# Attention scores of two heads issued side by side, with a ring of four for the split probabilities

## The chip, the cores and the metric

The kernel runs on one core of a Trainium2 chip. The metric is the time of one execution in microseconds. The engines that matter here are TensorE (PE in the profile; PEld is its weight load), VectorE (DVE), ScalarE (ACT), GpSimd (POOL) and the DMA queue that SyncE (SP) feeds. Each engine takes its instructions in the order in which they are written; semaphores tie the engines together.

## What is computed

One layer of a vision transformer over 32 images of 256x256 (the rows are the tokens), with a class token in front, so that 257 tokens of width 256 stand for an image:

- tokens: a three-level Haar transform, gates from dot products with all coefficients, and the inverse transform;
- attention with 16 heads of width 64: `qkv = layernorm(x) @ w_qkv`, rotary embedding on q and k, `scores = q @ k^T / sqrt(192)` plus a slope per head times the distance and a causal mask, softmax, `softmax @ v`, output projection, residual;
- a feed-forward part of width 1024 whose activations and weights are rounded to integers: `silu(gate) * up`, then `down`, residual.

```
scores = jnp.einsum('bhqd,bhkd->bhqk', q, k) / jnp.sqrt(jnp.float32(f))
...
out = bitlinear(silu(bitlinear(x, w_gate)) * bitlinear(x, w_up), w_down)
```

## The kernel before, in words

The first transposes XT start 147 us into the span; from there the program is a pipeline over images. A step works on four images at once: stage A makes the tokens of image s+1 (synthesis, layer norm, transposes XT), stage B the q, k and v of image s, stage C the attention of image s-1, stage E the output projection and the feed-forward part of image s-1. A step has 16 slots, k = 0 to 15, and each engine runs the same slots with its own share of each. Steps 4 to 29 are a hardware loop of 13 passes with two steps each; the others are written out.

The order is written by hand, by tables of slots: QK_SLOT = 1, 2, 3, 4, 5, 7, 8, 9 (one group of two head pairs of q or k each), V_SLOT = 10 to 13, SYN_SLOT = 6 (the synthesis of stage A, L774), OP_PARTS = slots 2 and 3 (output projection), H2_SLOT = 4 and XQ_SLOT = 5 (residual, layer norm and token scale on DVE), GU_SLOT = 7, 8, 10, 12 (gate and up), Q2T_SLOT = 11, 14, DOWN_SLOT = 14, 15.

One head of the attention takes this way, with k its slot:

- PE, slot k-2: `scores` (L706 to L714), two f32 matmuls of 64 rows each, 129 columns (the first 128 queries) and 257 columns (the other 128), into the bank `s_bank[h % 2]`. Even heads have their q and k on partitions 0 to 63, odd heads on 64 to 127. It waits (`t_done`) until DVE has evicted the two heads before.
- DVE, slot k-2: `ttr` (L1043), two instructions at L1055 that add the bias, write to `tp[:, h % 4]` and leave the maximum in `nm`. It waits for `s_ready`.
- ACT, slot k-2: `exps` (L501 on), two exponentials (L509) in place.
- PE, slot k: `transposes` (L720), three f32 transposes (L726) into one of the two banks `pt_bank`. ACT, slot k: `pt_hi` copies them to f16 (`ptr_h`, L514); DVE, slot k: `pt_lo` writes the f16 remainder (`ptr_l`, L1060). `ptr_h` and `ptr_l` have two buffers, `h % 2`.
- PE, slot k+1: `values` (L740), nine f16 matmuls of 64 columns (L624) into `o_bank`. It waits for `pt_free`, which `pt_lo` raises, and for the first head of a group of four for `ao_ready`.
- DVE, slots 4, 8, 12 and 0: `normalise` (L1070), the reciprocal (L1073) and the multiplication of four heads (L1079) out of `o_bank`. PE, slots 6, 10, 14 and 2: `out_transposes` (L731), four transposes of them (L735) through `pt_bank`.

The QK and V matmuls all use one bank, `b_bank`: the next group waits (`rq_ready`, `vl_done`) until ACT (L501, rows `rq`) or ACT and DVE (L560, L1169) have evicted the last. `output`, `quantise_tokens` (L1093 to L1104) and `norm_stats` (L1082) are further DVE work in the slots named. In a slot PE's order is: XT or synthesis, scores, QK or V, transposes of xq, transposes of the head, output projection, values, gate and up, `out_transposes`, down, transposes of q2.

Of the kernel before, what the change touches and what calls it, by code (L numbers as in the profile page):

```python
# [27 lines left out]
F16 = mybir.dt.float16  # L28
# [25 lines left out]
AHEAD = 2  # L54
BANDS, OPS, TERMS, BLOCK = 10, 4, 3, 8
# [52 lines left out]
def vit_layer(nc, x, cls_tok, Wa, ba, Wd1, bd1, Wd2, bd2, Wd3, bd3, w_qkv, b_qkv, w_out, b_out,  # L108
              w_gate, w_up, w_down, c_cos, c_sin, c_rel, c_mask, c_row, c_avg, c_eye, out):
    with ExitStack() as ctx:  # L110
# [69 lines left out]
        ptr_h = sb("ptr_h", [P, 2, 3, P], F16)  # L180
        ptr_l = sb("ptr_l", [P, 2, 3, P], F16)
# [317 lines left out]
        def _(act):  # L499
# [16 lines left out]
            def pt_hi(c, h, start):  # L516
                if not start or h >= 2:
                    act.wait_ge(pv_done, 16 * c + h - 1)
                use = pt_use(h, start)
                hi_of(c, use, ptr_h[:, h % 2], pt_bank[use % 2][:, 0:3 * P].rearrange("p (b n) -> p b n", b=3))  # L520
# [99 lines left out]
        def _(pe):  # L620
# [86 lines left out]
            def scores(c, h, par, start):  # L707
                half = slice(64 * (h % 2), 64 * (h % 2) + 64)
                if not start or h >= 2:
                    pe.wait_ge(t_done, 32 * c + 2 * h - 2)  # L710
                j = h // 2
                bank = s_bank[h % 2]
                pe.matmul(bank[:, 0:W0], qt[par][half, j, 0:P], kt[par][half, j, 0:W0], start=True, stop=True)  # L713
                pe.matmul(bank[:, W0:SCOLS], qt[par][half, j, P:SIDE], kt[par][half, j, :], start=True, stop=True).then_inc(s_ready, 1)  # L714
# [23 lines left out]
            def values(c, h, par, start):  # L738
# [6 lines left out]
                for t in range(T):  # L745
                    dst = o_bank[:, t * SIDE + (h % 4) * DH:t * SIDE + (h % 4 + 1) * DH]
                    blocks = [(0, 0)] if t == 0 else [(1, 0), (2, 1)]
                    for n, (pb, kb) in enumerate(blocks):
                        ins = split3(dst, (ptr_h[:, h % 2, pb, :], ptr_l[:, h % 2, pb, :]),
# [3 lines left out]
            def step(s, par):  # L753
# [3 lines left out]
                for k in range(SLOTS):  # L757
# [19 lines left out]
                    if ahead:  # L777
                        if ahead[1] == 0:
                            pe.wait_ge(qk_done, 8 * s + 8)
                        scores(ahead[0], ahead[1], par if ahead[1] < AHEAD else cp, ahead[2])  # L780

# [49 lines left out]
                    if has_c and k >= 1:  # L831
                        values(c, k - 1, cp, start)
                    if has_e and not start and k == 0:
                        values(c - 1, HEADS - 1, par, False)
# [37 lines left out]
        def _(dve):  # L872
# [189 lines left out]
            def pt_lo(c, h, start):  # L1062
                use = pt_use(h, start)
                lo_of(c, use, ptr_l[:, h % 2], pt_bank[use % 2][:, 0:3 * P].rearrange("p (b n) -> p b n", b=3), ptr_h[:, h % 2])
# [55 lines left out]
            def step(s, par):  # L1120
# [5 lines left out]
                for k in range(SLOTS):  # L1126
                    ahead = head_ahead(s, k)
                    if ahead:
                        ttr(*ahead)
                    if k == 0 and has_e and not start:  # L1130
# [47 lines left out]
                    if has_c and k >= 4 and k % 4 == 0:  # L1178
# [91 lines left out]
```

## Time and profile before

| | |
|---|---|
| median of 3 runs | 2515.66 us (2510.66 to 2520.93) |
| the profiled execution | 2511.47 us, of which span 2509.7 us |
| busy, share of the span | PE 84%, PEld 59%, DVE 70%, ACT 54%, POOL 41% |
| mean granted TensorE clock | 0.926 |

A step takes about 69 us, and 75 us where the loop turns back in it. A line of groups gives the line of the kernel, the engine, the operation, what it writes and reads, the count, the busy time, the mean of one in ns, and the idle time before it with what ended it. A matmul of f32 data shows as two records, and its end is modelled, so starts are the better measure of PE.

### The profile page before, as it was taken

To read this page: it belongs to the slowest core of one execution; us is meant where nothing else is said; L and a number is where in the kernel's file an instruction comes from. 1 tells how busy PE (TensorE), PEld (TensorE's weight loads), DVE (VectorE), ACT (ScalarE), POOL (GpSimd) and SP (SyncE) were. 2 spreads that over 40 slices of the span, in tenths; PEclk is the share of its full clock that TensorE was granted. 3 is DMA by queue.
4 is the path that set the end of the run, shared out by engine and by line. 5 is a ranking of instruction groups with operands and counts; after the bars stand their busy time and mean duration, and the time that the engine had idled before them with its cause. 6 is when DMAs were issued, how large, how long until landed. Compare 5 with 4: busy or idle time off the path is not lost.

```text
span 2509.7 us, 55124 instructions
## 1 busy us (share of the span) xinstructions
PE 2097.1 (84%) x16742; PEld 1478.4 (59%) x16742; DVE 1747.1 (70%) x5024; ACT 1366.7 (54%) x3841; POOL 1019.9 (41%) x1098
## 2 busy tenths in 40 slices
PE   3658889888888898888888888889888888888885
PEld 2535666666566665655656666656666655566653
DVE  2537777767777676768767676777767677777764
ACT  0125665556555555656656565655655565556653
POOL 0155543434455444434554353455534344554400
PEclk7789999999899999989999999899989999999976
DMA  7311111111111111111111111111111111111100
GB/s 174 122 47 39 44 48 43 39 39 44 36 39 47 49 46 38 41 36 37 43 48 48 38 45 36 39 38 45 47 43 40 38 43 39 39 47 43 43 9 9
DMA packets 98172, 114.84 MB, mean 46 GB/s; under 512 B 22721, under 2 KB 60066, under 8 KB 97570
## 3 DMA queue, kind: packets, MB, share of 16 engines
q1 hardware_dynamic: 97826, 110.61, 17.1%
q8 instruction: 170, 2.79, 0.5%
q14 instruction: 176, 1.44, 0.2%
HBM read 26.62 MB, written 8.42 MB: 14 GB/s over the span
## 4 chain that ended last, share of the span: by engine, by line
PE 38%; issue 23%; DVE 20%; ACT 9%; POOL 6%; SPq 2%; DVEq 1%; ACTq 0%; DMA 0%; POOLq 0%
PE bank L624 17%; PE bank L714 4%; PE bank L774 4%; PE bank L713 3%; PE bank L726 3%; DVE th L1202 2%; PE bank L858 2%; DVE arena L1206 2%; DVE es L1209 2%; ACT arena L509 2%; DVE ptr_l L1060 2%; DVE arena L1055 2%; POOL arena L484 2%; POOL rot L480 2%; PE bank L735 1%
## 5 line engine op out<-in xcount | busy, mean ns | idle before, releaser
L480 POOL TENSOR_TENSOR rot<-rot,sin 128x512 f32<-128x512 f32 x256 | 328.7, 1284 | 1176.4 <-DMA rot<-rq 1176.1
L509 ACT ACTIVATE arena<-arena,nm 128x129 f32<-128x129 f32 (+1 forms) x1024 | 458.4, 455 | 193.2 <-DVE nm L1055 192.9
L1055 DVE CUSTOM_DVE_ANT_0 arena<-bank,bias 128x129 f32<-128x129 f32 (+1 forms) x1024 | 323.9, 354 | 206.4 <-PE bank L714 190.8
L624 PE MATMUL bank<-xt_h,weights 128*128 128x256 f16 x2048 | 404.7, 285 | 8.4 <-ACT rq L501 5.8
L501 ACT ACTIVATE rq<-bank,bqk 128x256 f32<-128x256 f32 x512 | 214.8, 471 | 343.2 <-PE bank L624 337.0
L514 ACT ACTIVATE ptr_h<-bank 128x384 f16<-128x384 f32 x512 | 250.0, 488 | 220.3 <-PE bank L726 220.0
L484 POOL TENSOR_TENSOR arena<-arena,rot 128x256 f32<-128x256 f32 (+1 forms) x384 | 346.9, 918 | 30.3 <-POOL rot L480 0.5
L624 PE MATMUL bank<-arena,ptr_h 128*128 128x64 f16 x3072 | 215.0, 198 | 162.2 <-DVE ptr_l L1060 155.4
L1060 DVE TENSOR_TENSOR ptr_l<-bank,ptr_h 128x384 f16<-128x384 f32 x512 | 281.1, 549 | 55.5 <-ACT ptr_h L514 54.9
L714 PE MATMUL bank<-arena 64*128 64x257 f32 x1024 | 319.2, 393 | 0.0
L624 PEld LDWEIGHTS bank<-arena,ptr_h 128*128 128x128 f16 x3072 | 189.4, 101 | 195.2 <-DVE ptr_l L1060 181.6
L624 PE MATMUL bank<-xt_l,weights 128*128 128x256 f16 x1024 | 291.0, 284 | 0.0
L713 PE MATMUL bank<-arena 64*128 64x129 f32 x1024 | 258.3, 334 | 38.4 <-issue 36.4
L624 PEld LDWEIGHTS bank<-xt_h,weights 128*128 128x128 f16 x2048 | 207.3, 101 | 127.8 <-issue 85.9
L726 PE MATMUL bank<-eye,arena 128*128 128x128 f32 x1536 | 271.1, 287 | 0.0
L1174 DVE TENSOR_TENSOR arena<-rq,cos 128x256 f32<-128x256 f32 (+1 forms) x192 | 134.6, 727 | 173.2 <-ACT rq L501 173.2
L713 PEld LDWEIGHTS bank<-arena 64*128 64x128 f32 x1024 | 157.2, 192 | 148.3 <-issue 130.5
L726 PEld LDWEIGHTS bank<-eye,arena 128*128 128x128 f32 x1536 | 188.0, 146 | 77.4 <-issue 40.7
L624 PE MATMUL bank<-weights,xt_h 128*128 128x512 f16 x512 | 156.3, 387 | 58.1 <-DVE arena L1169 56.4
L509 ACT ACTIVATION_READ_ACCUMULATOR arena<-arena,nm 128x1 f32 x1024 | 202.2, 197 | 0.0
L624 PE MATMUL bank<-arena,ptr_l 128*128 128x64 f16 x1536 | 198.3, 198 | 0.0
L624 PE MATMUL bank<-weights,arena 128*128 128x256 f16 x1536 | 178.3, 273 | 1.9 <-DVE arena L1060 1.5
(187 smaller groups left out, 3766.2 us busy)
## 6 DMA issues: line engine op xcount, KB each, us to landing
rot<-rq SPq DMA_DIRECT2D x1024, 64.0 KB, 2.0
arena<-in_x SPq DMA_DIRECT2D x4, 2048.0 KB, 18.2
xin<-in_x SPq DMA_DIRECT2D x32, 256.0 KB, 2.7
hr<-hr SPq DMA_DIRECT2D x32, 256.0 KB, 2.4
out<-h SPq DMA_DIRECT2D x64, 128.0 KB, 1.7
arena<-in_L_attn_w_qkv SPq DMA_DIRECT2D x2, 1536.0 KB, 6.4
arena<-in_L_attn_w_out SPq DMA_DIRECT2D x1, 1024.0 KB, 10.1
arena<-in_L_ffn_w_gate SPq DMA_DIRECT2D x1, 1024.0 KB, 6.5
```

The source lines that it names most:

```text
L480: pool.tensor_tensor(r, r, sin[:, :].unsqueeze(1).broadcast_to([P, 2, SIDE]), ALU.mult).then_inc(t2_ready, 1)
L484: ins = pool.tensor_tensor(dst, dst, rot[:, g % 2, :, cols], ALU.add)
L501: return act.activation(dst, src, ACT.Identity, **kw)
L509: act.activation(cols, cols, ACT.Exp, bias=nm[:, t, h:h + 1], scale=-1.0, accum_out=rs[:, t, h:h + 1]).then_inc(e_done, 1)
L514: act.activation(dst, src, ACT.Copy).then_inc(hi_done, 1)
L624: ins = pe.matmul(dst, lhs[l], rhs[r], start=start and n == 0, stop=stop and n == len(parts) - 1)
L713: pe.matmul(bank[:, 0:W0], qt[par][half, j, 0:P], kt[par][half, j, 0:W0], start=True, stop=True)
L714: pe.matmul(bank[:, W0:SCOLS], qt[par][half, j, P:SIDE], kt[par][half, j, :], start=True, stop=True).then_inc(s_ready, 1)
L726: ins = pe.transpose(pt_bank[use % 2][:, n * P:(n + 1) * P], r[:, col:col + P], eye[:, :])
L1055: dve.tensor_tensor_reduce(r[:, cols], bank[:, cols], b, -1.0, 3.0e38, ALU.add, ALU.min, nm[:, t, h:h + 1]).then_inc(t_done, 1)
L1060: tt(dst, src, hi, ALU.subtract).then_inc(pt_free, 1)
L1174: ins = tt(dst, rq[:, g % 2, :, r], cos[:, r].unsqueeze(1).broadcast_to([P, 2, r.stop - r.start]), ALU.mult)
```

## The change

It has two parts. (1) `scores` becomes `score_pair`: in even slots PE issues both heads of a pair, 129 columns of each half and then 257 columns of each half, after one wait; DVE's `ttr` for both stands in the even slot too. ACT's exponentials stay one head a slot. (2) `ptr_h` and `ptr_l` have four buffers instead of two, `values` of head h stands in slot h+2 instead of h+1, and `normalise` moves one slot later, to 5, 9, 13 and 1. `out_transposes` stay in slots 6, 10, 14 and 2.

```diff
@@ -52,6 +52,7 @@
 V_SLOT = [10, 11, 12, 13]
 BEFORE_SYN = sum(k < SYN_SLOT for k in QK_SLOT)
 AHEAD = 2
+RING, LAG = 4, 2
 BANDS, OPS, TERMS, BLOCK = 10, 4, 3, 8
 FACTORS = OPS * TERMS
 Z_COLS = 4
@@ -177,8 +178,8 @@
         nm = sb("nm", [P, T, HEADS])
         rs = sb("rs", [P, T, HEADS])
         rinv = sb("rinv", [P, T, 4])
-        ptr_h = sb("ptr_h", [P, 2, 3, P], F16)
-        ptr_l = sb("ptr_l", [P, 2, 3, P], F16)
+        ptr_h = sb("ptr_h", [P, RING, 3, P], F16)
+        ptr_l = sb("ptr_l", [P, RING, 3, P], F16)
         ao = sb("ao", [P, 2, T, 4 * DH])
 
         h2 = sb("h2", [P, 2, T, SIDE])
@@ -514,10 +515,10 @@
                 act.activation(dst, src, ACT.Copy).then_inc(hi_done, 1)
 
             def pt_hi(c, h, start):
-                if not start or h >= 2:
-                    act.wait_ge(pv_done, 16 * c + h - 1)
+                if not start or h >= RING:
+                    act.wait_ge(pv_done, 16 * c + h - RING + 1)
                 use = pt_use(h, start)
-                hi_of(c, use, ptr_h[:, h % 2], pt_bank[use % 2][:, 0:3 * P].rearrange("p (b n) -> p b n", b=3))
+                hi_of(c, use, ptr_h[:, h % RING], pt_bank[use % 2][:, 0:3 * P].rearrange("p (b n) -> p b n", b=3))
 
             def at_hi(c, g, last=False):
                 if not first(c):
@@ -704,14 +705,14 @@
             pe.wait_ge(prep_done, 1)
             pe.wait_ge(turned_copied, 6)
 
-            def scores(c, h, par, start):
-                half = slice(64 * (h % 2), 64 * (h % 2) + 64)
-                if not start or h >= 2:
-                    pe.wait_ge(t_done, 32 * c + 2 * h - 2)
-                j = h // 2
-                bank = s_bank[h % 2]
-                pe.matmul(bank[:, 0:W0], qt[par][half, j, 0:P], kt[par][half, j, 0:W0], start=True, stop=True)
-                pe.matmul(bank[:, W0:SCOLS], qt[par][half, j, P:SIDE], kt[par][half, j, :], start=True, stop=True).then_inc(s_ready, 1)
+            def score_pair(c, j, par, start):
+                halves = slice(0, 64), slice(64, 128)
+                if not start or j >= 1:
+                    pe.wait_ge(t_done, 32 * c + 4 * j)
+                for half, bank in zip(halves, s_bank):
+                    pe.matmul(bank[:, 0:W0], qt[par][half, j, 0:P], kt[par][half, j, 0:W0], start=True, stop=True)
+                for half, bank in zip(halves, s_bank):
+                    pe.matmul(bank[:, W0:SCOLS], qt[par][half, j, P:SIDE], kt[par][half, j, :], start=True, stop=True).then_inc(s_ready, 1)
 
             def wait_bank(c, use, start):
                 if not start or use >= 2:
@@ -746,7 +747,7 @@
                     dst = o_bank[:, t * SIDE + (h % 4) * DH:t * SIDE + (h % 4 + 1) * DH]
                     blocks = [(0, 0)] if t == 0 else [(1, 0), (2, 1)]
                     for n, (pb, kb) in enumerate(blocks):
-                        ins = split3(dst, (ptr_h[:, h % 2, pb, :], ptr_l[:, h % 2, pb, :]),
+                        ins = split3(dst, (ptr_h[:, h % RING, pb, :], ptr_l[:, h % RING, pb, :]),
                                      (vh[par][:, kb, feat], vl[par][:, kb, feat]), n == 0, n == len(blocks) - 1)
                 ins.then_inc(pv_done, 1)
 
@@ -774,10 +775,10 @@
                             ins = pe.matmul(b_bank[:, :], rowop[:, o, :], rhs, start=o == 0, stop=o == OPS - 1)
                         ins.then_inc(syn_ready, 1)
                     ahead = head_ahead(s, k)
-                    if ahead:
+                    if ahead and k % 2 == 0:
                         if ahead[1] == 0:
                             pe.wait_ge(qk_done, 8 * s + 8)
-                        scores(ahead[0], ahead[1], par if ahead[1] < AHEAD else cp, ahead[2])
+                        score_pair(ahead[0], ahead[1] // 2, par if ahead[1] < AHEAD else cp, ahead[2])
 
                     if has_b and k in QK_SLOT:
                         g = QK_SLOT.index(k)
@@ -828,10 +829,10 @@
                                              (wo_h[:, j, :], wo_l[:, j, :]), j == 0, j == PAIRS - 1)
                         if k == 3:
                             ins.then_inc(op_ready, 1)
-                    if has_c and k >= 1:
-                        values(c, k - 1, cp, start)
-                    if has_e and not start and k == 0:
-                        values(c - 1, HEADS - 1, par, False)
+                    if has_c and k >= LAG:
+                        values(c, k - LAG, cp, start)
+                    if has_e and not start and k < LAG:
+                        values(c - 1, HEADS - LAG + k, par, False)
                     if has_e and k in GU_SLOT:
                         n = GU_SLOT.index(k)
                         t, half = n // 2, n % 2
@@ -1061,7 +1062,7 @@
 
             def pt_lo(c, h, start):
                 use = pt_use(h, start)
-                lo_of(c, use, ptr_l[:, h % 2], pt_bank[use % 2][:, 0:3 * P].rearrange("p (b n) -> p b n", b=3), ptr_h[:, h % 2])
+                lo_of(c, use, ptr_l[:, h % RING], pt_bank[use % 2][:, 0:3 * P].rearrange("p (b n) -> p b n", b=3), ptr_h[:, h % RING])
 
             def at_lo(c, g, last=False):
                 feat = slice(2 * g, 2 * g + 2)
@@ -1125,8 +1126,9 @@
                 ce.begin(e)
                 for k in range(SLOTS):
                     ahead = head_ahead(s, k)
-                    if ahead:
+                    if ahead and k % 2 == 0:
                         ttr(*ahead)
+                        ttr(*head_ahead(s, k + 1))
                     if k == 0 and has_e and not start:
                         output(e - 1, 1 - ep, 1)
                     if has_e and k - 1 == DOWN_SLOT[0]:
@@ -1175,9 +1177,9 @@
                         ins.then_inc(t1_done, 1)
                     if has_c:
                         pt_lo(c, k, start)
-                    if has_c and k >= 4 and k % 4 == 0:
+                    if has_c and k >= 4 and k % 4 == LAG - 1:
                         normalise(c, k // 4 - 1)
-                    if has_e and not start and k == 0:
+                    if has_e and not start and k == LAG - 1:
                         normalise(c - 1, 3)
 
                     if has_a and k == SYN_SLOT:
```

The built program shows what this does on PE around slots 4 and 5 of a step (L713 and L714, now L713 and L715, are score matmuls; L726, now L727, transposes of a head; `bank<-arena,ptr_h` and `ptr_l` values; `xt_h` and `xt_l` the q and k projection; REGISTER_ALU rows prepare a wait). Before, from the transposes of slot 4 to the projection of slot 5:

```order
L726 MATMUL bank<-eye,arena 128x128 x3
L739 REGISTER_ALU
L624 MATMUL bank<-arena,ptr_h 128x64 x2
L624 MATMUL bank<-arena,ptr_l 128x64
L624 MATMUL bank<-arena,ptr_h 128x64 x2
L624 MATMUL bank<-arena,ptr_l 128x64
L624 MATMUL bank<-arena,ptr_h 128x64 x2
L624 MATMUL bank<-arena,ptr_l 128x64
L710 REGISTER_ALU
L713 MATMUL bank<-arena 128x129
L714 MATMUL bank<-arena 128x257
L789 REGISTER_ALU
```

Now, from the last values of slot 3 to the projection of slot 4, and then the boundary from slot 4 to slot 5:

```order
L625 MATMUL bank<-arena,ptr_l 128x64
L625 MATMUL bank<-arena,ptr_h 128x64 x2
L625 MATMUL bank<-arena,ptr_l 128x64
L711 REGISTER_ALU
L713 MATMUL bank<-arena 128x129 x2
L715 MATMUL bank<-arena 128x257 x2
L790 REGISTER_ALU
L625 MATMUL bank<-xt_h,weights 128x256
```

```order
L727 MATMUL bank<-eye,arena 128x128 x3
L625 MATMUL bank<-arena,ptr_h 128x64 x2
L625 MATMUL bank<-arena,ptr_l 128x64
L625 MATMUL bank<-arena,ptr_h 128x64 x2
L625 MATMUL bank<-arena,ptr_l 128x64
L625 MATMUL bank<-arena,ptr_h 128x64 x2
L625 MATMUL bank<-arena,ptr_l 128x64
L790 REGISTER_ALU
L625 MATMUL bank<-xt_h,weights 128x256
```

The scores of head 7 have left the boundary and stand with those of head 6 in front of the projection of slot 4, so that in slot 5 the projection follows the values directly.

On DVE, slots 4 and 5 (L1055, now L1056, is the eviction of scores; L1060, now L1061, `ptr_l`; L1096, now L1097, the start of the token scale). Before, from the normalisation's neighbour to the token scale:

```order
L1059 REGISTER_ALU
L1060 TENSOR_TENSOR ptr_l<-bank,ptr_h 128x384
L1072 ISA
L1073 RECIPROCAL rinv<-rs 128x8
L1078 REGISTER_ALU
L1079 TENSOR_TENSOR ao<-bank,rinv 128x512
L1046 REGISTER_ALU
L1055 ISA arena,nm<-bank,bias 128x129
L1055 ISA nm 128x1
L1055 ISA arena,nm<-bank,bias 128x257
L1055 ISA nm 128x1
L1096 TENSOR_SCALAR th<-h,mv,rstd 128x256 x2
```

Now the residual follows two evictions, and the token scale follows `ptr_l`:

```order
L1056 ISA arena,nm<-bank,bias 128x257
L1056 ISA nm 128x1
L1047 REGISTER_ALU
L1056 ISA arena,nm<-bank,bias 128x129
L1056 ISA nm 128x1
L1056 ISA arena,nm<-bank,bias 128x257
L1056 ISA nm 128x1
L1155 SCALAR_TENSOR_TENSOR h<-bank,hr 128x512
```

```order
L1060 REGISTER_ALU
L1061 TENSOR_TENSOR ptr_l<-bank,ptr_h 128x384
L1097 TENSOR_SCALAR th<-h,mv,rstd 128x256 x2
L85 REGISTER_ALU
L1099 TENSOR_REDUCE es<-th 128x2
```

The second eviction has moved ahead of the residual (L1153, now L1155), and the normalisation from in front of the token scale to behind it, beside the evictions of slot 6.

## Rows read from the trace of the kernel before

**Rows 1.** Page: busy time of the engines; the chain by engine.
```profile
PE 2097.1 (84%) x16742; PEld 1478.4 (59%) x16742; DVE 1747.1 (70%) x5024; ACT 1366.7 (54%) x3841; POOL 1019.9 (41%) x1098
...
PE 38%; issue 23%; DVE 20%; ACT 9%; POOL 6%; SPq 2%; DVEq 1%; ACTq 0%; DMA 0%; POOLq 0%
```

**Rows 2.** Stretches of one step: window, length, busy us of PE, PEld, DVE, ACT, POOL; clock, DMA.
```profile
1187.92:1203.79 15.87, 15.87 (x153) 13.25 (x153) 8.91 (x28) 8.44 (x29) 6.51 (x5) 1.00 0.29 79
1203.79:1210.14 6.35, 5.86 (x59) 4.63 (x57) 4.87 (x19) 3.05 (x10) 4.47 (x4) 1.00 0.20 46
1210.14:1216.51 6.37, 5.87 (x29) 2.95 (x29) 6.20 (x14) 2.43 (x10) 5.20 (x6) 1.00 0.38 93
...
1221.45:1253.41 31.96, 26.02 (x205) 17.31 (x205) 27.42 (x76) 20.69 (x57) 13.53 (x17) 0.95 0.11 25
...
1259.97:1266.80 6.83, 6.83 (x32) 4.69 (x33) 3.05 (x12) 1.36 (x5) 0.00 (x0) 0.50 0.18 62
```

**Rows 3.** PE in order of time: start, us, engine, line, operation, count.
```profile
1197.07 0.19 PE L624 MATMUL bank<-arena,ptr_l 128*128 128x64 f16 x1
1197.09 0.63 PE L735 MATMUL bank<-eye,ao 128*128 128x128 f32 x4
...
1203.67 0.19 PE L624 MATMUL bank<-arena,ptr_l 128*128 128x64 f16 x1
1203.79 0.49 PE L713 MATMUL bank<-arena 64*128 64x129 f32 x2
1204.12 0.60 PE L714 MATMUL bank<-arena 64*128 64x257 f32 x2
1204.64 0.28 PE L624 MATMUL bank<-xt_h,weights 128*128 128x256 f16 x1
...
1205.97 0.49 PE L726 MATMUL bank<-eye,arena 128*128 128x128 f32 x3
...
1210.14 1.12 PE L774 MATMUL bank<-xin,rowop 128*128 128x512 f32 x2 [0.49 <-ACT rq L501]
```

**Rows 4.** The chain of waits through the same step: start, us, what.
```profile
1210.14 3.69 PE bank L774 x8
...
1256.91 3.05 issue
1259.96 0.57 PE bank L713
```

**Rows 5.** ACT in order of time.
```profile
1206.17 0.84 ACT L501 ACTIVATE rq<-bank,bqk 128x256 f32<-128x256 f32 x2 [3.89 <-PE bank L624]
```

**Rows 6.** DVE in order of time.
```profile
1204.93 0.29 DVE L1055 CUSTOM_DVE_ANT_0 arena<-bank,bias 128x129 f32<-128x129 f32 x1 [1.93 <-PE bank L714]
...
1205.49 0.69 DVE L1153 SCALAR_TENSOR_TENSOR h<-bank,hr 128x512 f32<-128x512 f32 x1
...
1208.08 0.19 DVE L1073 RECIPROCAL rinv<-rs 128x8 f32<-128x8 f32 x1
...
1209.00 0.28 DVE L1055 CUSTOM_DVE_ANT_0 arena<-bank,bias 128x129 f32<-128x129 f32 x1
...
1209.55 0.73 DVE L1096 TENSOR_SCALAR th<-h,mv,rstd 128x256 f32<-128x256 f32 x2
...
1215.07 0.54 DVE L1060 TENSOR_TENSOR ptr_l<-bank,ptr_h 128x384 f16<-128x384 f32 x1
...
1242.89 0.69 DVE L1169 SCALAR_TENSOR_TENSOR arena<-bank,arena 128x512 f16<-128x512 f32 x1 [1.18 <-ACT arena L560]
```

**Rows 7.** PE at the step's end, in order of time.
```profile
1249.72 0.29 PE L624 MATMUL bank<-arena,ptr_h 128*128 128x64 f16 x2 [1.87 <-DVE ptr_l L1060]
...
1252.79 0.79 PE L865 MATMUL bank<-eye,q 128*128 128x128 f16 x8
...
1255.86 1.05 PE L858 MATMUL bank<-wdn,q2t 128*128 128x256 f16 x8 [0.26 <-ACT q2t L543]
```

**Rows 8.** Waits over the whole span: us in total, times, longest.
```profile
PE bank L624 <- DVE ptr_l L1060: 155.4, 88, 2.8
```

## The prediction, made before the changed kernel was run

> **What bounds the kernel now.** I read the page's busy shares and chain first. PE is busy 84% and DVE 70% of the span, and the chain that ended last is PE for 38%, DVE for 20% and "issue" for 23% [rows 1]: the two take turns. So I cut one step of the steady state into stretches [rows 2]. In slots 0 to 3 (1187.92 to 1203.79) PE is busy all of its 15.87 us while DVE works 8.91: a saved PE microsecond is a saved microsecond. In slots 4 and 5 PE still has 5.86 of 6.35. From the synthesis to slot 7 DVE works 6.20 of 6.37, beside 5.87 of PE. In slots 8 to 14 DVE works 27.42 of 31.96 and PE waits in pieces; there PE time is worth little, and what matters is what stands in DVE's queue ahead of what PE and ACT wait for. The step here is 69.0 us (slot 0 to slot 0, 1187.92 to 1256.92), then comes the loop's turn with 3.05 us in which nothing runs [rows 4].
>
> **What a score set costs.** The last value matmul in front of a set starts at 1203.67, at a pace of 0.03; the first projection behind it starts at 1204.64 [rows 3]. So a head costs PE 1204.64 - 1203.70 = 0.94 us. The pure streaming is less: the synthesis takes 3.69 us for 8 records of 512 columns [rows 4], 0.90 ns a column and record, and a head has 2 x (129 + 257) = 772 of them: 0.69 us. The other 0.25 is entering and leaving. What that is shows by its neighbour: four f32 transposes over all 128 rows follow the last value matmul after 0.02 us (1197.07 to 1197.09), the 64-row scores only after 0.12 (1203.67 to 1203.79), and behind them stands a gap of the same kind [rows 3]. The Trainium skill, "TensorEngine Tiling (Array Packing)", section Tiling Modes, says that a change of tiling mode drains the array and a change of tile does not; the trace agrees as far as the mode goes, and shows no change of tile alone.
>
> A pair costs 1.88 now. Bounds for it after the change:
> - At least the entering and leaving of one head goes: 0.25 saved. That is the end without any overlap of the two halves. Below it the trace gives nothing but the gap: if each of the three changes of half costs the 0.1 of that gap, nothing is saved.
> - At most the second head disappears behind the first: 0.94 saved.
> I take 0.55. Each matmul is two records on the same 64 rows, in the order A A B B (129 columns), A A B B (257): only where a record of one half follows one of the other can they overlap, which is 0.12 + 0.12 + 0.23 of the 0.69; weights have to be loaded between them too, so I take 0.3 of it, plus 0.25.
> The Trainium skill, "TensorE: Matmul & The Clock Gate", Part 3, says that matmuls in different row groups run together with starts about 4 ns apart. By that rule the pair would come near the 0.94 end, which is the third rival below; no row here shows two halves next to each other.
>
> **The sum for one step,** in the order of time, gains positive.
> - Slots 0 to 3: two pairs, 2 x 0.55 = **+1.1**. With all of it PE-bound, it arrives. The output projection waits for DVE's remainder of the last `out_transposes`, which keeps its distance.
> - Slot 5: new wait. The projection there needs ACT's eviction of the slot before, which starts 0.2 after the projection ends (1205.97 to 1206.17) and takes 0.84 [rows 3, 5]. Now only transposes and values (about 0.6) stand between, no scores: PE stops for 0.4. The third pair in slot 4 pays it (0.55), and the synthesis waits for its own eviction as now (0.49) [rows 3].
> - Slots 4 to 7, DVE: **-0.9**. The residual (1205.49) now stands behind a second eviction of 0.56 (1204.93 to 1205.49), whose scores also end later. In front of the token scale the normalisation (1208.08 to 1209.00, 0.92) and one eviction (0.55) are gone, but it needs POOL's root, so it starts at about the same distance, and it ends with the `ptr_l` of 1215.07 [rows 6]. Then the 0.92 of the normalisation stands in front of the evictions of slot 6, hence of ACT's exponentials and its rounding of the tokens behind them. PE's values and `out_transposes` in slot 6 wait for it too, about as long as PE now waits there for `ptr_l`.
> - Slots 8 to 13, DVE-bound: **-0.2**. The normalisation moves from slot 8, where ACT's exponentials and tanh hid it, into slot 9 and delays the first V remainder by 0.9. In slot 11 no eviction stands ahead of the second one any more, and the wait of 1.18 for the third [rows 6] shrinks to about half: 0.7 comes back.
> - Slots 14 and 15: **+0.5**. Values now wait for a `ptr_l` that is long done, so the stop of 1.87 at 1249.72 [rows 7] goes. In its place `out_transposes` wait for the normalisation, now in slot 13 and about 2 us after the inner scale, where this `ptr_l` is 1.7 after it; but DVE's evictions and `q2` go on meanwhile, and the transposes of q2 (1252.79) start about 0.5 earlier.
> - Slot 15 loses a whole score set on PE, and that is worth **0**: the down product behind it already waits 0.26 for ACT's copy of q2t [rows 7], and will wait 1.2.
> Sum: 1.1 - 0.9 - 0.2 + 0.5 = 0.5 us a step, 16 us over 32 steps. After the loop's turn PE's granted clock is 0.50, the 1.2 GHz level, for 6.83 us [rows 2], in which the first pair falls, so there it saves twice as much: 13 turns x 0.55 = 7 us. From the profiled execution's own 2511.5 us (span 2509.7 and 1.8 around it; the median of the runs, 2515.7, is 4 higher) that gives 2488; I say **2490 us**. With the pair at 0.25 the first term is 0.5 and the step -0.1; with 0.94 it is 1.9 and the step 1.3: 2511 to 2463 with little or nothing from the turns.
>
> **Rivals.**
> - *The halves take turns* (the pair saves 0.25 or nothing). For it: no row shows two matmuls of 64 rows overlapping, and f32 matmuls come as two dependent records. Against: nothing in the trace. Then the gain of slots 0 to 3 is eaten by slots 4 to 7: -0.1 a step, about 2512 us. No change.
> - *Evictions in pairs get in DVE's way* (slower). The place is DVE's queue in slots 4, 8, 10 and 12, where 0.56 of the next head's eviction, not needed before ACT's next slot, stands ahead of work that PE and ACT wait for, together with 0.92 of normalisation in slots 9 and 13. For it: 27.42 of 31.96 busy there. Against: total work on DVE is unchanged, and what is done early is not done later. If half of the four evictions (1.1) shows on top of my -0.2 and the end gives 0 instead of 0.5, the step is 1.1 lower than my sum: 1.1 - 0.9 - 1.3 = -1.1, and the pairs of the loop's turn give 7 back: about 2539 us at worst, 2530 as its middle. It decides as soon as these delays exceed 0.5 a step.
> - *Both parts give more.* The halves overlap nearly in full, 1.9 in slots 0 to 3 and slots 4 to 6 follow, and the waits of values for `ptr_l`, 155.4 us in 88 pieces [rows 8], leave the path in other places than slot 14 too. For it: values are what PE stops for most. Against: most of those pieces lie where DVE is the bound, and PE only stops for something else. At 2 us a step: 2445 us.
>
> **How the numbers follow.** Forecast 0.33, turns 0.23, slower 0.22, more 0.22. What this measurement can tell from no change is about 0.5%, 12.6 us: faster is below 2503, slower above 2528. Faster: 0.29 of the forecast, all of the third rival, 0.02 of the first: 0.53. Same: 0.04 + 0.18 + 0.02 of the slower one = 0.24. Slower: 0.23. The forecast's own range is 2463 to 2511. The range of 8 in 10 reaches down to the third rival and up to the middle of the slower one with a little more: 2432 to 2534.
>
> **What would show it.** The starts in slot 4: from the last value matmul to the first projection about 1.36 us for two heads (1.67 if they take turns, 1.0 if in full overlap). In slot 5 a stop of PE for ACT's `rq` of about 0.4. The row of values waiting for `ptr_l` falls from 155 us to near nothing, and rows of `out_transposes` or values waiting for `ao` grow. The evictions of slot 6 come about 1.5 after the token scale's end instead of at once. In slot 15 the down product waits about 1.2 for q2t. DVE's and ACT's busy times stay. I am wrong if slots 0 to 3 don't get shorter by about 1, or if slots 8 to 14, now 32 us, change by more than 1 in either direction; and if PE, with longer stops, is granted 1.2 GHz more often than the 0.95 of the last stretch [rows 2] shows now.

## The result, and the profile after

The changed kernel takes 2550.8 us (median of 4, 2550.3 to 2555.0) against 2518.3 us before (2510.7 to 2526.5): a ratio of 1.013, interval 1.010 to 1.017. It is slower, where 2490 us and faster was forecast, and 17 us above the range. Its two parts taken alone pull in opposite directions: the pairs alone give 2418 us, the lag alone (values two slots behind, normalisation one slot later) 2609 us. The two don't add up: -3.7% and +3.7% are no change, and +1.3% was measured.

The page, in the order of [rows 1]:

```profile
PE 1940.9 (76%) x16742; PEld 1399.2 (55%) x16742; DVE 1797.6 (71%) x5024; ACT 1373.3 (54%) x3841; POOL 1028.5 (40%) x1098
...
issue 49%; POOL 21%; DVE 15%; PE 9%; ACT 2%; SPq 2%; POOLq 1%; DMA 1%; DVEq 0%; ACTq 0%
```

PE does the same 16742 matmuls in 156 us less busy time, and the kernel is slower all the same. The chain reads quite differently from [rows 1] (PE 9%, "issue" 49%, POOL 21%). Half of it names no wait, so I do not use it as a guide. DVE does the same 5024 instructions in 50 us more, though its busy time was forecast to stay; more on this below. The stretches of one step are (slots 0 to 3, 4 and 5, synthesis to slot 8, slot 8 to XT):

```profile
1209.09:1223.06 13.97, 13.97 (x154) 12.23 (x153) 8.39 (x26) 8.43 (x29) 5.44 (x4) 1.00 0.30 80
1223.06:1228.97 5.91, 5.00 (x59) 4.17 (x57) 4.21 (x16) 3.05 (x10) 4.62 (x5) 1.00 0.18 42
1228.97:1242.14 13.17, 10.81 (x64) 6.39 (x64) 10.18 (x28) 7.00 (x20) 8.37 (x9) 0.87 0.20 51
1242.14:1276.73 34.59, 27.15 (x210) 17.95 (x209) 29.02 (x81) 20.97 (x57) 13.63 (x17) 0.81 0.10 23
```

Against [rows 2]: slots 0 to 3 went from 15.87 to 13.97 us, 1.9 less, and slots 4 and 5 from 6.35 to 5.91. Then the gain is given back, with interest: slot 8 to XT had 31.96 and has 34.59 now, 2.6 more, and its granted clock fell from 0.95 to 0.81. From synthesis to slot 8 it is 13.17 against 11.31 (1210.14 to 1221.45), 1.9 more, at 0.87.

Where it happens is plain on PE in slot 10 of a step. Before the change, with the V product of slot 11 at the end:

```profile
1232.75 0.23 PE L624 MATMUL bank<-arena,ptr_h 128*128 128x64 f16 x2 [2.00 <-DVE ptr_l L1060]
...
1233.02 1.03 PE L845 MATMUL bank<-wgu,xqt 128*128 128x512 f16 x4
...
1236.09 0.61 PE L624 MATMUL bank<-weights,xt_h 128*128 128x512 f16 x2 [0.76 <-DVE arena L1169]
...
1237.40 0.49 PE L726 MATMUL bank<-eye,arena 128*128 128x128 f32 x3
```

and after it:

```profile
1250.23 0.49 PE L727 MATMUL bank<-eye,arena 128*128 128x128 f32 x3
1254.19 0.27 PE L625 MATMUL bank<-arena,ptr_h 128*128 128x64 f16 x2 [3.47 <-DVE ao L1080]
...
1254.64 1.90 PE L846 MATMUL bank<-wgu,xqt 128*128 128x512 f16 x4
...
1258.21 1.04 PE L625 MATMUL bank<-weights,xt_h 128*128 128x512 f16 x2 [0.82 <-DVE arena L1171]
...
1260.74 0.85 PE L727 MATMUL bank<-eye,arena 128*128 128x128 f32 x3
```

The values of head 8 wait 3.47 us for `ao`, the normalisation of heads 4 to 7. After it PE works at half clock: the gate and up products take 1.90 instead of 1.03, the V product of slot 11 takes 2.53 (1258.21 to 1260.74) instead of 1.31 (1236.09 to 1237.40). The granted clock of the stretch is 0.50, the 1.2 GHz level:

```profile
1254.19:1260.74 6.55, 5.73 (x23) 2.75 (x24) 6.48 (x17) 2.16 (x6) 5.61 (x6) 0.50 0.00 0
```

The trace has 29 steps that can be compared. The V product of slot 11 is that slow in 20 of them; in the other 9 it takes 1.31 behind stops for `ao` that are as long (3.6 to 4.0 us). In the kernel before it is slow in 2 of 29.

And DVE, which is busy throughout, shows why `ao` is late and for whom it is in the way. From the second gate product to the first V remainder, before and after:

```profile
1227.52 0.68 DVE L1202 SCALAR_TENSOR_TENSOR th<-th,bank 128x512 f32<-128x512 f32 x1
...
1235.36 0.68 DVE L1169 SCALAR_TENSOR_TENSOR arena<-bank,arena 128x512 f16<-128x512 f32 x1
```

```profile
1248.18 0.69 DVE L1204 SCALAR_TENSOR_TENSOR th<-th,bank 128x512 f32<-128x512 f32 x1 [0.26 <-ACT th L592]
...
1251.30 1.35 DVE L1176 TENSOR_TENSOR arena<-rq,cos 128x256 f32<-128x256 f32 x2
1252.58 0.55 DVE L1061 TENSOR_TENSOR ptr_l<-bank,ptr_h 128x384 f16<-128x384 f32 x1
1253.04 0.19 DVE L1074 RECIPROCAL rinv<-rs 128x8 f32<-128x8 f32 x1
1253.35 0.69 DVE L1080 TENSOR_TENSOR ao<-bank,rinv 128x512 f32<-128x512 f32 x1
...
1257.47 0.68 DVE L1171 SCALAR_TENSOR_TENSOR arena<-bank,arena 128x512 f16<-128x512 f32 x1
...
1261.68 0.69 DVE L1171 SCALAR_TENSOR_TENSOR arena<-bank,arena 128x512 f16<-128x512 f32 x1 [0.43 <-ACT arena L561]
...
1264.21 0.29 DVE L1056 CUSTOM_DVE_ANT_0 arena<-bank,bias 128x129 f32<-128x129 f32 x1 [1.37 <-PE bank L715]
```

The normalisation stands behind a whole gate product, its scale and the cosine; the first V remainder comes after it; and then DVE itself waits, 0.43 for the V product (by way of ACT's copy of it) and 1.37 for scores that PE made slowly. The stretch from gate product to V remainder was 7.84 us (1227.52 to 1235.36) and is 9.29 (1248.18 to 1257.47). The normalisation is 0.92 of the difference. The rest is mostly two instructions that were there before and run longer now, the cosine product (1.35 instead of 1.00) and the scaling of `xn` behind it (1.68 instead of 1.13). Over the span it is these, and the start of the token scale, that make up DVE's 50 us. The cosine product goes from a mean of 563 to 688 ns; the others, first before and then after:

```profile
L1096 DVE TENSOR_SCALAR th<-h,mv,rstd 128x256 f32<-128x256 f32 x66 | 44.9, 721 | 1.7 <-POOL rstd L462 1.0
...
L1189 DVE TENSOR_SCALAR xn<-hh,mv,rstd 128x256 f32<-128x256 f32 x64 | 42.5, 704 | 0.9 <-POOL rstd L465 0.9
```

```profile
L1097 DVE TENSOR_SCALAR th<-h,mv,rstd 128x256 f32<-128x256 f32 x66 | 62.6, 989 | 20.0 <-POOL rstd L463 20.0
L1191 DVE TENSOR_SCALAR xn<-hh,mv,rstd 128x256 f32<-128x256 f32 x64 | 61.5, 1001 | 0.9 <-POOL rstd L466 0.9
```

Why they run longer no run shows.

The stops for `ao` are in 3 of 4 groups of heads. Over the span (PE's waits):

```profile
PE bank L625 <- DVE ao L1080: 304.3, 96, 6.1
```

The 155 us of values waiting for `ptr_l` [rows 8] have left PE's list and 304 us for `ao` are there instead: 96 of them, three a step.

The pair itself does better than forecast. The scores of slot 0, four records to a row:

```profile
1209.09 0.49 PE L713 MATMUL bank<-arena 64*128 64x129 f32 x4
1209.41 0.60 PE L715 MATMUL bank<-arena 64*128 64x257 f32 x4
1209.94 0.55 PE L727 MATMUL bank<-eye,arena 128*128 128x128 f32 x3
```

0.85 us from the first score to what follows, for two heads. One head took 0.85 as well (1203.79 to 1204.64 [rows 3]). The second half is free. Between the last value matmul and the projection of slot 4 lie 0.99 us for two heads, where I had forecast 1.36, and 1.0 for full overlap.

### The profile page after: what moved, and what is told of

Its sections match the earlier page's. It is cut to its first block, busy times and chain, and to the rows that moved or that the text cites. A ratio compares the mean times of both kernels' runs of the same rounds, so it can differ in the third digit from the quotient of the medians.

```text
span 2548.2 us, 54966 instructions
## 1 busy us (share of the span) xinstructions
PE 1940.9 (76%) x16742; PEld 1399.2 (55%) x16742; DVE 1797.6 (71%) x5024; ACT 1373.3 (54%) x3841; POOL 1028.5 (40%) x1098
## 3 DMA queue, kind: packets, MB, share of 16 engines
q14 instruction: 176, 1.44, 0.2%
## 4 chain that ended last, share of the span: by engine, by line
issue 49%; POOL 21%; DVE 15%; PE 9%; ACT 2%; SPq 2%; POOLq 1%; DMA 1%; DVEq 0%; ACTq 0%
POOL rot L481 7%; POOL arena L485 5%; PE bank L625 4%; POOL arena L476 3%; POOL rowop L451 1%; POOL hr L492 1%; DVE ptr_l L1061 1%; DVE th L1097 1%; DVE arena L1056 1%; PE bank L659 1%; DVE es L1100 1%; DVE es L1103 1%; SPq L353 1%; DVE es L1099 1%; POOL rstd L463 1%
## 5 line engine op out<-in xcount | busy, mean ns | idle before, releaser
L481 POOL TENSOR_TENSOR rot<-rot,sin 128x512 f32<-128x512 f32 x256 | 348.2, 1360 | 1162.3 <-DMA rot<-rq 1161.7
L1056 DVE CUSTOM_DVE_ANT_0 arena<-bank,bias 128x129 f32<-128x129 f32 (+1 forms) x1024 | 305.1, 354 | 181.7 <-PE bank L715 172.1
L625 PE MATMUL bank<-xt_h,weights 128*128 128x256 f16 x2048 | 407.9, 287 | 21.2 <-ACT rq L502 18.3
L625 PEld LDWEIGHTS bank<-arena,ptr_h 128*128 128x128 f16 x3072 | 201.8, 104 | 332.6 <-DVE ptr_l L1061 147.8
L485 POOL TENSOR_TENSOR arena<-arena,rot 128x256 f32<-128x256 f32 (+1 forms) x384 | 332.2, 879 | 30.3 <-POOL rot L481 0.5
L1061 DVE TENSOR_TENSOR ptr_l<-bank,ptr_h 128x384 f16<-128x384 f32 x512 | 281.5, 550 | 21.1 <-ACT ptr_h L515 19.6
L727 PE MATMUL bank<-eye,arena 128*128 128x128 f32 x1536 | 273.4, 289 | 1.5 <-DVE ptr_l L1061 1.5
L1176 DVE TENSOR_TENSOR arena<-rq,cos 128x256 f32<-128x256 f32 (+1 forms) x192 | 146.5, 790 | 152.3 <-ACT rq L502 152.3
L727 PEld LDWEIGHTS bank<-eye,arena 128*128 128x128 f32 x1536 | 192.9, 149 | 71.5 <-issue 46.5
L625 PE MATMUL bank<-weights,xt_h 128*128 128x512 f16 x512 | 172.4, 422 | 58.5 <-DVE arena L1171 51.8
L625 PE MATMUL bank<-arena,ptr_l 128*128 128x64 f16 x1536 | 207.4, 202 | 0.0
L476 POOL TENSOR_TENSOR arena<-rq,cos 128x256 f32<-128x256 f32 (+1 forms) x192 | 176.5, 933 | 0.0
L846 PE MATMUL bank<-wgu,xqt 128*128 128x512 f16 x528 | 162.0, 437 | 5.3 <-DVE th L1204 1.9
L625 PEld LDWEIGHTS bank<-weights,arena 128*128 128x128 f16 x1536 | 148.9, 98 | 20.1 <-DVE arena L1061 3.1
```

The lines of the kernel that those rows point to most:

```text
L476: ins = pool.tensor_tensor(dst, rq[:, g % 2, :, cols], cos[:, cols].unsqueeze(1).broadcast_to([P, 2, cols.stop - cols.start]), ALU.mult)
L481: pool.tensor_tensor(r, r, sin[:, :].unsqueeze(1).broadcast_to([P, 2, SIDE]), ALU.mult).then_inc(t2_ready, 1)
L485: ins = pool.tensor_tensor(dst, dst, rot[:, g % 2, :, cols], ALU.add)
L625: ins = pe.matmul(dst, lhs[l], rhs[r], start=start and n == 0, stop=stop and n == len(parts) - 1)
L727: ins = pe.transpose(pt_bank[use % 2][:, n * P:(n + 1) * P], r[:, col:col + P], eye[:, :])
L846: ins = pe.matmul(bank[:, :], xqt[:, kc, t * P:(t + 1) * P], wgu[:, kc, base + half * 512:base + (half + 1) * 512], start=kc == 0, stop=kc ...
```

## The experiments

All times are medians of 4 or more runs; the kernel before, run beside them, had 2510 us (with pairs_only, lag_only, norm_early, single_evictions), 2521 (pairs_single_evictions, one_normalisation_early, filled_stops, pair_halves_in_turn) and 2518 (the others). Ratios are to it, as they are on record; they differ by up to 0.4% from the quotient of the medians. Differences in us between kernels that did not run side by side carry the few us by which the kernel before moved.

**The two parts apart, the normalisation, the evictions**

```diff
-RING, LAG = 4, 2      # pairs_only
+RING, LAG = 2, 1
```

> The paired scores and paired evictions stay; values, buffers and normalisation are as before the change (RING, LAG = 2, 1). My theory (late normalisation): the changed kernel is slow because the normalisation of four heads moved one slot later on VectorE, the values of the next four heads wait for it (304 us of stops before values for ao), and TensorE falls to 1.2 GHz in those stops; without the lag the 1.9 us a step that the pairs gave in slots 0 to 3 should show: 2475 to 2500 us, the stops for ao near zero, mean clock back to 0.92. Rival (evictions in pairs are in VectorE's way): the pairing itself is the loss, and this stays near 2540 us.

Measured: **2417.7 us, 0.963 (0.958 to 0.967)**, clock 0.944. Below even what the late-normalisation theory gave. Its step is 3.3 us shorter than that of the kernel before, and only 1.9 of this lie from XT to the next synthesis, where the pairs of slots 0 to 3 save PE time. Another 1.3 come between the first V remainder and XT (means over 29 steps, in the table further down): there DVE reaches the second V remainder without an eviction in front of it, as the prediction had said of slot 11.

`lag_only`: `score_pair` and the two `ttr` in a row go back to one head a slot; ring, lag and normalisation are as changed.

> Scores and evictions one head a slot as before the change; values two slots behind with four buffers, normalisation one slot later. Late normalisation: the loss stands alone here, 2550 to 2590 us, with the stops before values for ao of about 300 us and a mean clock under 0.90. Rival (evictions in pairs): with them gone this is near the kernel before, 2505 to 2525 us.

Measured: **2608.7 us, 1.037 (1.033 to 1.041)**, clock 0.897. That is above the 2550 to 2590 us expected, with fewer stops for `ao` (225 us, not 300). The loss is in the lag part, and the rival falls.

```diff
-                    if has_c and k >= LAG:
-                        values(c, k - LAG, cp, start)
+                    if has_c:              # norm_early; heads_of(4) = [2, 3], (5) = [], (6) = [4], (7) = [5]
+                        for h in heads_of(k):
+                            values(c, h, cp, start)
...
-                    if has_c and k >= 4 and k % 4 == LAG - 1:
+                    if has_c and k >= 4 and k % 4 == 0:
                         normalise(c, k // 4 - 1)
```

> The changed kernel, but the values of heads 3, 7, 11 and 15 run one slot behind (so slot 4, 8, 12 and 0 do two heads' values, and slots 1, 5, 9 and 13 none), and the normalisation is back in slots 4, 8, 12 and 0. Pairs, four buffers and the lag of the other heads stay. Late normalisation: 2450 to 2490 us, stops for ao under 100 us, clock 0.92. Rival (evictions in pairs): 2535 to 2550 us, since VectorE's queue still has both evictions in front.

Measured: **2452.5 us, 0.976 (0.972 to 0.980)**, clock 0.894. Of the 133 us between the changed kernel and pairs_only, 98 come back when the normalisation does, together with the values of every fourth head; 35 stay with the lag of the others. The clock stayed low, against the expectation.

```diff
-                    if ahead and k % 2 == 0:      # single_evictions, on VectorE
+                    if ahead:
                         ttr(*ahead)
-                        ttr(*head_ahead(s, k + 1))
```

> The changed kernel, but VectorE evicts one head a slot as before; TensorE still issues the scores in pairs. Late normalisation: little changes, 2535 to 2552 us. Rival (evictions in pairs are in VectorE's way): 2490 to 2515 us.

Measured: **2567.3 us, 1.019 (1.014 to 1.025)**. Evicting in pairs is not the loss: taking it away does not help. That it costs 16 us more is not certain, since the two ratios' intervals overlap (1.014 to 1.025, and 1.010 to 1.017 for the changed kernel). The same edit on pairs_only:

> As pairs_only, but VectorE evicts one head a slot; TensorE still issues scores in pairs. With the changed kernel this edit cost 16 us (2567 against 2551), with TensorE stopping 278 us for nm in front of the pairs. If the paired eviction is a gain of its own, by letting TensorE's next pair start on time: 2430 to 2450 us. If that cost came from the late normalisation alone: 2400 to 2420 us.

Measured: **2573.6 us, 1.019 (1.015 to 1.024)**: 156 us more than pairs_only, far outside both expectations. Its list of PE's waits has the reason:

```profile
PE bank L713 <- DVE nm L1056: 247.6, 96, 3.3
```

The next pair needs both banks, and with one eviction a slot the second is read only in the slot directly ahead of it, on an engine that runs behind PE. So evictions in pairs belong to scores in pairs; against evictions one by one with scores one by one, no run holds them alone.

**Do the places add up?** `one_normalisation_early`: of the four normalisations only that of slot 9 goes back to slot 8, with the values of head 7.

> The changed kernel with one of its four normalisations moved back: that of heads 4 to 7 stands in slot 8 again, with the values of head 7 one slot behind; the other three stay in 5, 13 and 1. From the traces, the stretches that hold slots 5, 9 and 13 are each 1.2 us longer with the late normalisation than with the early one (norm_early against the changed kernel). If the three places add up: 1.2 x 32 = 38 us less than the changed kernel, 2505 to 2520 us. If only the last one matters because the loss is carried from place to place: 2540 to 2555 us. If it is all in slot 9, where the clock falls: 2450 to 2470 us.

Measured: **2530.0 us, 1.003 (0.9998 to 1.006)**: 21 us less than the changed kernel. That is about half of the 38 us of full addition, more than nothing, and much less than if all of it were in slot 9. The trace shows where the other half went. From the first gate product to the first V remainder DVE takes 13.0 us instead of 14.4 (means over 29 steps), and from there to XT 18.9 instead of 18.3.

**The clock.** Matmuls of no use keep PE busy while it would stand. The bank they write (`g_bank`) is free there, after a wait that the cut below leaves out, and is overwritten:

```diff
+FILL = {4: 6, 8: 12, 12: 10}            # filled_stops; norm_early_filled {8: 10, 12: 8}
+            def fill(n):
+                for _ in range(n):
+                    pe.matmul(g_bank[:, :], eye16[:, :], wgu[:, 0, 0:512], start=True, stop=True)
             def values(c, h, par, start):
+                if h in FILL:
+                    ...
+                    fill(FILL[h])
```

> The changed kernel with matmuls of no use (512 columns, their result is overwritten) in front of the values of heads 4, 8 and 12: 6, 12 and 10 of them, 1.3, 2.6 and 2.2 us at 2.4 GHz, each less than the stop for ao at that place (2.05, 3.47 and 2.93 us in the changed kernel's trace). They take no wait away. Theory (the clock is part of the loss): TensorE keeps 2.4 GHz behind the stops, the V product of slot 11 takes 1.3 instead of 2.5 us and the down product 1.05 instead of 1.9, mean granted clock above 0.92, and the time falls by 1.5 to 3 us a step: 2455 to 2500 us. Rival (the clock falls but nothing on the chain runs then, only the late normalisation counts): 2540 to 2560 us.

Measured: **2488.9 us, 0.986 (0.981 to 0.990)**, clock 0.942. 62 us come back by adding work. The V product of slot 11 is slow in 8 of 29 steps instead of 20. All of the gain lies behind the first V remainder: from there to XT a step takes 16.4 us instead of 18.3 (means), and 1.9 us times 32 steps are 61. The late normalisation is still in it (stops for `ao` 111 us), and the kernel is still 71 us slower than pairs_only, at the same mean clock.

> norm_early (2452 us) with 10 and 8 matmuls of no use of 512 columns in front of the values of heads 8 and 12 (2.2 and 1.7 us). norm_early and pairs_only differ by 35 us though VectorE needs the same 12.4 us from the first gate to the first V remainder in both. Theory (the lag runs the short stops of TensorE together into one long one, after which the V product of slot 11 runs at 1.2 GHz): with the stop filled, 2415 to 2435 us, close to pairs_only. Rival (the lag costs by its order alone, for instance two heads' values in one slot): 2445 to 2460 us.

Measured: **2409.6 us, 0.958 (0.952 to 0.964)**, clock 0.924: 43 us less, and no more than pairs_only. What the lag does is seen at slot 11 of norm_early, PE and then DVE:

```profile
1214.33 0.66 PE L742 MATMUL bank<-eye,ao 128*128 128x128 f32 x4 [1.60 <-DVE ptr_l L1069]
1217.71 1.04 PE L631 MATMUL bank<-weights,xt_h 128*128 128x512 f16 x2 [2.72 <-DVE arena L1179]
...
1220.25 0.65 PE L733 MATMUL bank<-eye,arena 128*128 128x128 f32 x3
```

```profile
1204.59 0.69 DVE L1212 SCALAR_TENSOR_TENSOR th<-th,bank 128x512 f32<-128x512 f32 x1 [0.59 <-ACT th L598]
...
1216.97 0.68 DVE L1179 SCALAR_TENSOR_TENSOR arena<-bank,arena 128x512 f16<-128x512 f32 x1
```

and in pairs_only:

```profile
1191.48 0.22 PE L625 MATMUL bank<-arena,ptr_h 128*128 128x64 f16 x2 [1.42 <-DVE ao L1080]
...
1195.92 0.23 PE L625 MATMUL bank<-arena,ptr_h 128*128 128x64 f16 x2 [1.44 <-DVE ptr_l L1061]
...
1199.30 0.60 PE L625 MATMUL bank<-weights,xt_h 128*128 128x512 f16 x2 [1.64 <-DVE arena L1171]
...
1200.61 0.49 PE L727 MATMUL bank<-eye,arena 128*128 128x128 f32 x3
```

```profile
1186.19 0.69 DVE L1204 SCALAR_TENSOR_TENSOR th<-th,bank 128x512 f32<-128x512 f32 x1 [0.60 <-ACT th L592]
...
1198.56 0.68 DVE L1171 SCALAR_TENSOR_TENSOR arena<-bank,arena 128x512 f16<-128x512 f32 x1
```

DVE takes 12.38 us from the first gate to the first V remainder with the lag and 12.37 without: it is the bound, and the lag buys nothing there. PE stops in both. Without the lag it does so three times for 1.4 to 1.6 us, and the V product takes 1.31 us (1199.30 to 1200.61). With it PE runs ahead and stands twice, 1.60 and 2.72 us, almost back to back, and the V product takes 2.54. In norm_early it does so in 29 of 29 steps, in pairs_only in 1 of 29.

`pairs_filled` fills only the stop of slot 14 of pairs_only (`FILL = {13: 9}`), `before_filled` that of the kernel before (`{13: 8}`).

> pairs_only (2418 us) with 9 such matmuls (1.9 us) in front of the values of head 13 in slot 14, where TensorE stops 2.2 us for ptr_l. If the clock behind that stop matters: 2395 to 2412 us. If the clock was held there anyway in most steps: 2412 to 2425 us.

Measured: **2392.8 us, 0.952 (0.946 to 0.958)**: the fastest kernel of this study, 28 us under pairs_ring4, which ran beside it and equals pairs_only. It is also 17 us under norm_early_filled, which ran beside it too, with other stops filled. So about half of the lag's 35 us is left when both have filled stops, and the clock is not shown to be all of its cost.

> The kernel before the change, with 8 such matmuls (1.7 us) in front of the values of head 13 in slot 14, where it stops 1.9 us and the clock falls in the step shown before the prediction. A control for the three filled kernels. Theory (only a fallen clock is bought back): this one has little of it, so 2500 to 2515 us against 2515. If filling helped by something else than the clock, this would fall by 30 us or more as the changed kernel did.

Measured: **2488.2 us, 0.989 (0.985 to 0.992)**: 30 us less, at the limit that I had set for "something else"; the kernel before had more to buy back than I thought. Its mean clock, 0.918, is no higher than before (0.926), and the clock fell elsewhere. The down product behind the filled stop, in the kernel before and then filled, and the V product, likewise:

```profile
L858 PE MATMUL bank<-wdn,q2t 128*128 128x256 f16 x528 | 84.9, 315 | 10.4 <-ACT q2t L543 8.8 <-DVE arena L1206 1.6
...
L624 PE MATMUL bank<-weights,xt_h 128*128 128x512 f16 x512 | 156.3, 387 | 58.1 <-DVE arena L1169 56.4 <-ACT rq L501 1.7
```

```profile
L866 PE MATMUL bank<-wdn,q2t 128*128 128x256 f16 x528 | 70.4, 278 | 10.9 <-ACT q2t L544 9.2 <-DVE arena L1214 1.6
...
L625 PE MATMUL bank<-weights,xt_h 128*128 128x512 f16 x512 | 166.2, 409 | 27.0 <-DVE arena L1177 25.5 <-ACT rq L502 1.5
```

The down product went from 315 to 278 ns a matmul, the V product from 387 to 409: that of slot 11 is slow in 13 of 29 steps instead of 2. So a mean over the span does not show what filling does; it counts where the clock is low. That these 30 us are all clock is not shown, and the same doubt stands for the other filled kernels. In the changed kernel and in norm_early the mean rose as well, from 0.878 to 0.942 and from 0.894 to 0.924.

**How the two halves share the array**

```diff
                 for half, bank in zip(halves, s_bank):
                     pe.matmul(bank[:, 0:W0], ...)
-                for half, bank in zip(halves, s_bank):
                     pe.matmul(bank[:, W0:SCOLS], ...)
```

> As pairs_only, but the four matmuls of a pair in the order 129 and 257 columns of the even head, then 129 and 257 columns of the odd head. Theory A (TensorE takes matmuls strictly in order and only neighbours on different halves overlap): the first 257 columns overlap the second 129 at most, a pair takes 0.44 us longer than in pairs_only (0.85), and slots 0 to 3 make the kernel 25 to 40 us slower: 2440 to 2460 us. Theory B (each half works through its own matmuls, whatever their order): a pair still takes 0.85 us and the time is that of pairs_only, 2410 to 2425 us.

Measured: **2424.2 us, 0.958 (0.954 to 0.963)**, the ratio of pairs_only. Theory B holds: in the trace the four records of 129 columns start together at 1204.80 again and those of 257 at 1205.12, though the order was 129, 257, 129, 257.

```profile
1204.80 0.50 PE L713 MATMUL bank<-arena 64*128 64x129 f32 x4
1205.12 0.61 PE L714 MATMUL bank<-arena 64*128 64x257 f32 x4
```

**The buffers**, `RING, LAG = 4, 1`:

> pairs_only with four buffers for ptr_h and ptr_l instead of two, values still one slot behind: the buffers alone. ACT waits for a value product before it writes ptr_h in neither trace to speak of, so nothing changes: 2410 to 2425 us. If ACT's copies were held back by the two buffers: 2380 to 2405 us.

Measured: **2421.0 us, 0.964 (0.957 to 0.970)**: nothing, as expected.

## Why the prediction was wrong

Means over 29 steps of each trace, in us. Gate means DVE's first gate product, V its first V remainder:

| | synthesis to gate | gate to V | V to XT | XT to next synthesis | step |
|---|---|---|---|---|---|
| before | 13.40 | 12.71 | 17.28 | 28.33 | 71.72 |
| changed | 15.06 | 14.43 | 18.29 | 25.24 | 73.02 |
| filled_stops | 14.88 | 14.12 | 16.38 | 25.51 | 70.89 |
| norm_early | 13.75 | 13.03 | 17.45 | 25.46 | 69.70 |
| norm_early_filled | 13.41 | 12.45 | 16.00 | 26.70 | 68.56 |
| pairs_only | 13.29 | 12.69 | 15.95 | 26.47 | 68.41 |

The forecast, in these stretches, was +0.9, +0.9, -1.2 and -1.1. Measured are +1.7, +1.7, +1.0 and -3.1.

- *Slots 0 to 3, +1.1*: right in place, too small. A pair costs one head, so the saving is the full 0.94 that I had as the upper end, and the stretch is 1.9 shorter. I had put records in one line (A A B B) and let only neighbours overlap; the order does not matter (`pair_halves_in_turn`). Here the rule in the Trainium skill, "TensorE: Matmul & The Clock Gate", Part 3, that different row groups run together, came nearer than my sum.
- *Slot 5, a stop of 0.4 for `rq`*: it came, 0.34 us. The stretch of slots 4 and 5 is 0.44 shorter, where one free head (0.94) less 0.4 gives 0.54.
- *Slots 4 to 7, -0.9*: the mechanism, normalisation ahead of the evictions, was right, the size was not. Of the 1.9 that the stretch from the synthesis to slot 8 lost, about half is this. The stop of values (2.05 us) was named too, as "about as long as PE now waits for `ptr_l`"; that was 0.50 there, and the stop was followed by 1.2 GHz.
- **The step that failed: slots 8 to 13, -0.2, and 14 and 15, +0.5.** Measured for slot 8 to XT: -2.6 against +0.3 or so. Two things were wrong in it. First, the delay of the first V remainder: 0.9 was forecast for the normalisation and came, but 1.7 were measured, mostly because other DVE instructions ran longer with it. Second, what was to come back behind the first V remainder, 0.7 in slots 11 and 12 and 0.5 at the end. I had taken PE's work at 2.4 GHz throughout, its V product at 1.3 us. Behind the stop of 3.47 it took 2.53, so the second remainder waits for it (0.43), and so do the next scores (1.37); the wait for the third did shrink to about half, 1.18 to 0.64, as forecast. From V to XT a step is 1.0 longer instead of 1.2 shorter. With the stops filled it is 0.9 shorter, so this second part is the clock's. I had written that 1.2 GHz after longer stops would make me wrong and gave it no price and no rival of its own; filled_stops puts it at 62 us of the changed kernel.
- The clock is the smaller part of the loss. Of the 98 us between the changed kernel and norm_early, 79 remain when both have their stops filled (filled_stops and norm_early_filled). They lie ahead of the V remainder: +1.5 and +1.7 us a step in the first two columns, with 1.2 given back in the fourth.
- *Slot 14*: removing the stop for `ptr_l` was counted as a gain. A stop for `ao` of 2.93 us took its place in that step. *Slot 15, 0*: right; the down product waits 1.25 us for q2t, as forecast (1.2).
- *The slower rival* had the right sign and one right half. The normalisation was its smaller part. The paired evictions, its larger one, are no loss: with scores in pairs, going back to single evictions costs 156 us in pairs_only, and does not help in the changed kernel. *The rival "more"* was right about the array and wrong about the lag: the values' stops for `ptr_l` went, and the kernel with the lag alone is slower.
- The errors partly cancel: in the first three stretches the kernel lost 3.8 us a step more than forecast, in the fourth it gained 2.0 more.
- Not settled: why the scaling of `xn`, the cosine product and the token scale run longer with the late normalisation; how the 79 us divide between that, the normalisation's own place and PE's stops; and what the lag costs beside the clock.

## What to carry to other kernels

Letting one engine run further ahead of the engine that bounds it gained nothing over the step here and collected its short stops into a long one; on TensorE that one was followed by work at half clock, which the bounding engine then had to wait for in most steps. When a step moves by a slot, look at what else stands in its new slot of the queue, and who waits behind it: here that cost more than the clock did. And split a change of two parts before judging it: here one was worth -3.7% and the other +3.7%, and together they were worth +1.3%.

## What the runs showed of the hardware

- Two f32 matmuls of 64 rows each, on the two halves of the partitions and into different banks, ran in the time of one: 0.85 us for 2 x 386 columns. In the other order of issue the records have the same starts and lengths (0.50 and 0.61 us, 0.32 apart).
- Stops of 1.42, 1.44 and 1.64 us with work between them left PE's V product at 2.4 GHz (1.31 us); it is so in 28 of 29 steps of pairs_only, with stops of 1.2 to 2.1 us. Stops of 1.60 and 2.72 close together were followed by 1.2 GHz (2.54 us); norm_early has such a pair of stops and the slow product in 29 of 29 steps. A stop of 3.47 was followed by it too (2.53 us), but stops of that kind (3.5 to 4.1 us) in only 20 of 29 steps of the changed kernel.
- Adding 28 useless matmuls a step made the changed kernel 62 us faster; 9 a step made the best one some 25 us faster. The down product behind slot 14 takes 1.6 to 1.7 us from its start to what follows in all 30 steps of the changed kernel and in 15 of 30 of the kernel before. With the stop ahead of it filled it takes 0.9 in all 30 of both.
- DVE's scaling of `xn`, the same 64 instructions of 128x256 f32, took 704 ns on average before and 1001 ns in the changed kernel (695 in pairs_only). No run shows why.
